# Attention kernel on one core: GpSimd adds the bias to the scores that come back from DRAM, VectorE takes their maximum

## What is computed

```python
def _L0_attn_ref(hidden_states, w_qkv, w_o):
    qkv = hidden_states @ w_qkv
    ...
    scores = jnp.einsum('bqhgd,bkhd->bhgqk', q, k) * scale
    bias = -slopes[:, :, None, None] * sqrt_dist
    bias = jnp.where(rel[None, None] >= 0, bias, -jnp.inf)
    attn = jax.nn.softmax(scores + bias[None], axis=-1)
    out = jnp.einsum('bhgqk,bkhd->bqhgd', attn, v).reshape(B, S, NH * D)
    return out @ w_o

x = x + _L0_attn_ref(_layernorm(x), w_qkv, w_o)
x = x + _L0_ffn_ref(_layernorm(x), weight, bias, centroids, assignments)
```

## Time and profile before

| | us |
|---|---|
| median of 3 executions (1272.35 to 1277.04) | 1273.97 |
| the profiled execution, device time | 1272.32 |
| the same, span of its trace | 1270.7 |
| TensorE's matmuls busy | 1238.5 (97%) |
| VectorE busy | 787.2 (62%) |
| ScalarE busy | 751.9 (59%) |
| GpSimd busy | 520.2 (41%) |

### The profile page before, as it was taken

One profiled execution on the slowest core, in us unless ns is written; L12 is line 12 of the kernel. 1 busy time (PEld: TensorE's weight loads), 2 busy tenths in 40 slices (PEclk: granted clock), 3 DMA queues, 4 the chain that ended last, 5 costly groups with the idle time before them and its releaser, 6 DMA issues.

```text
span 1270.7 us, 21113 instructions
## 1 busy us (share of the span) xinstructions
PE 1238.5 (97%) x5880; PEld 1029.3 (81%) x5880; DVE 787.2 (62%) x2086; ACT 751.9 (59%) x2171; POOL 520.2 (41%) x476
## 2 busy tenths in 40 slices
PE   9899999999999999999999999999999999999988
PEld 8688878887788878887888878888788878888777
DVE  7777656566555565656565566555655566668577
ACT  5776566565555656665556656664566566556443
POOL 4422636226342545226352455325452364233213
PEclk9899999999999999999999999999999999999999
DMA  5543535444453444444443444534444444523203
GB/s 199 178 132 123 161 119 182 140 135 142 152 173 123 141 160 154 157 140 132 165 155 118 161 160 149 166 124 149 142 155 149 138 160 154 168 83 116 92 9 133
DMA packets 205530, 180.71 MB, mean 142 GB/s; under 512 B 12096, under 2 KB 158784, under 8 KB 205504
## 3 DMA queue, kind: packets, MB, share of 16 engines
q1 hardware_dynamic: 199680, 162.04, 38.8%
q0 software_dynamic: 5824, 18.36, 4.9%
HBM read 101.45 MB, written 78.91 MB: 142 GB/s over the span
## 4 chain that ended last, share of the span: by engine, by line
issue 34%; PE 31%; POOL 21%; DVE 5%; ACT 4%; DMA 4%; POOLq 1%; SPq 0%; DVEq 0%; ACTq 0%
PE ps L1385 29%; POOL ring L592 11%; POOL wqkv_lo L551 2%; POOL wo_lo L551 2%; POOL v_lo L598 2%; POOL wqkv_hi L549 2%; ACT prob L765 1%; DMA vT<-turned_s 1%; PE ps L1405 1%; DMA turned<-ring_whole 1%; POOL wo_hi L549 1%; ACT prob L777 1%; POOL raw L557 1%; POOL raw L560 1%; DVE vT L1083 1%
## 5 line engine op out<-in xcount | busy, mean ns | idle before, releaser
L1385 PE MATMUL ps<-xnT,wqkv_hi 128*128 (+2 forms) x1560 | 483.3, 391 | 1.7 <-DVE kT L1005 1.3
L592 POOL TENSOR_TENSOR ring<-ring_whole,pT_hi 128x512 fp32r<-128x512 f32 x189 | 246.1, 1302 | 522.3 <-ACT pT_hi L756 522.0
L1385 PEld LDWEIGHTS ps<-xnT,wqkv_hi 128*128 128x128 f32 x1560 | 289.2, 188 | 67.4 <-DVE kT L1005 6.1
L1385 PE MATMUL ps<-xnT,wqkv_lo 128*128 (+1 forms) x780 | 303.3, 389 | 0.0
L765 ACT ACTIVATE prob<-prob,negmax 128x256 f32<-128x256 f32 (+1 forms) x384 | 177.1, 463 | 187.5 <-DVE negmax L1083 187.5
L1385 PE MATMUL ps<-wo_hi,oT_hi 128*128 128x512 f32 x512 | 200.1, 391 | 0.8 <-DVE acc L1062 0.8
L1385 PE MATMUL ps<-wo_lo,oT_hi 128*128 128x512 f32 x512 | 199.6, 390 | 0.0
L1385 PE MATMUL ps<-wo_hi,oT_lo 128*128 128x512 f32 x512 | 199.2, 389 | 0.0
L756 ACT ACTIVATE pT_hi<-ring_whole 128x512 fp32r<-128x512 f32 x189 | 118.0, 625 | 129.9 <-DMA ring_whole<-turned 88.3
L1062 DVE TENSOR_TENSOR acc<-ps,acc 128x512 f32 (+1 forms) x128 | 88.2, 690 | 146.6 <-PE ps L1385 146.2
L1385 PEld LDWEIGHTS ps<-xnT,wqkv_lo 128*128 128x128 f32 x780 | 146.9, 188 | 30.8
(11 more groups left out here) (155 smaller groups left out, 1788.4 us busy)
## 6 DMA issues: line engine op xcount, KB each, us to landing
turned<-ring_whole SPq DMA_DIRECT2D x189, 256.0 KB, 2.1
ring_whole<-turned SPq DMA_DIRECT2D x189, 256.0 KB, 2.9
turned_v<-vT SPq DMA_DIRECT2D x32, 256.0 KB, 2.0
...
```

The source lines that it names most:

```text
L592: pool.tensor_tensor(ring_slot(c), whole_slot(c), pT_hi[:, c % 2, :].bitcast(F32), ALU.subtract).then_inc(pT_lo_done, 1)
L1385: ins = pe.matmul(dst, l, r, start=start and m == 0, stop=stop and m == n - 1)
```

## The change

**GpSimd adds, VectorE takes the maximum.** For part 2 (`e` = 2 and 5) VectorE's four fused instructions go. GpSimd's new `sum_scores(u, b)` adds the bias in place to the returned piece, 128x512 in one instruction, and VectorE's new `find_max(u, b)` takes the four negated maxima in one `tensor_reduce`. Since the piece now has its own sign, `exps` for these parts has scale 1.0. GpSimd does `sum_scores(u, 0)` after `v_lo_part(u)` (in a fourth unit between the splits of the second and the third chunk of `w_qkv`), and `sum_scores(u - 1, 1)` between `pT_lo(1)` and `pT_lo(2)` of `body(u)`.

**Loads.** The loads of the third and fourth chunk of `w_qkv` go from GpSimd to SyncE. SyncE's loop over units becomes one over groups, with the two loads around `scores_in(v, 0)` of the fourth unit. Each waits until the slot is split. They have semaphores of their own.

**Orders.** VectorE: `find_max(u - 1, 1)` stands behind `turn(4)`, and `invert_sums(3)` follows it, ahead of `proj_lo(2)`; `turn(5)` goes behind `proj_lo(3)`. ScalarE: in unit 1 alone `pT_hi(0)` goes ahead of `exps(3)` and `exps(4)`; in the tail `pT_hi(1)` and `pT_hi(2)` move up, each ahead of a `normalise`. VectorE in the tail: the piece of `b = 1` is taken up after `dense_part(1, 1, 1)` and not ahead of `dense_part(1, 1, 0)`.

The diff, cut to its core (the rest declares semaphores and calls these functions in the first units, on the same pattern):

```diff
             def turn_first(v):
                 scores_out(v, 0)
                 scores_in(v, 0)
+                turn_rest(v)
+
+            def turn_rest(v):
                 scores_out(v, 1)
...
+            def last_qkv(g, c):
+
+                sp.wait_ge(raw_split, g * (2 * NC) + c - 1)
+                rows = w_qkv[c * P:(c + 1) * P, :]
+                kv = rows[:, NH * D:].rearrange("p (a n) -> p a n", a=2)[:, :, bass.ds(g * D, D)]
+                sp.dma_start(raw[:, c % 2, 0:HPG * D], rows[:, bass.ds(g * (HPG * D), HPG * D)]).then_inc(last_loaded[c % 2], 16)
+                sp.dma_start(raw[:, c % 2, HPG * D:QKV_W].rearrange("p (a n) -> p a n", a=2), kv).then_inc(last_loaded[c % 2], 16)
+
+            def unit(v):
+                turn_v(v)
+                turn_first(v)
+                turn_second(v)
+
+            def last_of_group(g):
+                v = g * QUADS + QUADS - 1
+                turn_v(v)
+                scores_out(v, 0)
+                last_qkv(g + 1, 2)
+                scores_in(v, 0)
+                last_qkv(g + 1, 3)
+                turn_rest(v)
+                turn_second(v)
...
-            with sp.Fori(1, UNITS - 3) as v:
-                turn_v(v)
-                turn_first(v)
-                turn_second(v)
+            for v in range(1, QUADS - 1):
+                unit(v)
+            last_of_group(0)
+            with sp.Fori(1, NKV - 1) as g:
+                for q in range(QUADS - 1):
+                    unit(g * QUADS + q)
+                last_of_group(g)
+            unit(UNITS - QUADS)
...
@@ split_qkv @@
                     if c == 2:
                         v_lo_part(g * QUADS - 1)
-
-                    pool.wait_ge(raw_loaded[c % 2], g * 96 - 96 + 32 * (c // 2 + 1))
+                        sum_scores(g * QUADS - 1, 0)
+
+                    if c < 2:
+                        pool.wait_ge(raw_loaded[c % 2], g * 64 - 32)
+                    else:
+                        pool.wait_ge(last_loaded[c % 2], g * 32)
                     split(raw[:, c % 2, :], wqkv_hi[:, c, :], wqkv_lo[:, c, :], g * (2 * NC) + SETUP + c + 1)
-                    if c < 2:
-                        load_after(g, c)
...
+            def sum_scores(u, b):
+
+                pool.wait_ge(s_in[b], u * 16 + 16)
+                pool.wait_ge(bias_ready, group_count(u))
+                by_head = score_tile(b).rearrange("p (i h c) -> p h i c", i=P // BLK, h=HPG)
+                pool.tensor_tensor(by_head, by_head, bias[:, :, P:SEQ].rearrange("p h (i c) -> p h i c", c=BLK),
+                                   ALU.add).then_inc(scores_summed, 1)
+
+            def pT_lo_first(u):
+                pT_lo_part(u, 0)
+                pT_lo_part(u, 1)
+                sum_scores(u - 1, 1)
+                pT_lo_part(u, 2)
...
             def plain_body(u):
-                for c in range(CHUNKS):
+                pT_lo_first(u)
+                for c in range(3, CHUNKS):
                     pT_lo_part(u, c)
                 v_lo_part(u)
+                sum_scores(u, 0)
...
@@ group @@
                     pT_lo_part(u + 1, h)
+                    if h == 1:
+                        sum_scores(u, 1)
...
@@ ScalarE @@
-                    ins = act.activation(s, s, ACT.Exp, bias=negmax[:, n:n + 1], scale=-1.0, accum_out=rowsum[:, n:n + 1])
+                    ins = act.activation(s, s, ACT.Exp, bias=negmax[:, n:n + 1], scale=1.0 if e % 3 == 2 else -1.0,
+                                         accum_out=rowsum[:, n:n + 1])
...
                 if attn:
+                    if is_second(u):
+                        pT_hi_part(u, 0)
                     exps(u - 1, 3)
                     exps(u - 1, 4)
-                    pT_hi_part(u, 0)
+                    if not is_second(u):
+                        pT_hi_part(u, 0)
...
@@ ScalarE, tail @@
             pT_hi_part(u, 0)
+            pT_hi_part(u, 1)
             normalise(u - 1, 2)
             exps(u - 1, 5)
-            pT_hi_part(u, 1)
+            pT_hi_part(u, 2)
             normalise(u - 1, 3)
             oT_hi_part(u, 0)
-            pT_hi_part(u, 2)
...
@@ VectorE @@
+            def find_max(u, b):
+
+                dve.wait_ge(scores_summed, u * 2 + b + 1)
+                n = 4 * (2 * b + 1)
+                dve.tensor_reduce(negmax[:, n:n + HPG], score_tile(b).rearrange("p (i h c) -> p h i c", i=P // BLK, h=HPG),
+                                  AX_XY, ALU.max, negate=True).then_inc(scores_biased, 1)
...
                     if attn and i == 0:
                         invert_sums(u - 1, 2)
-                        add_bias(u - 1, 5)
+                    if attn and i == 2:
+                        invert_sums(u - 1, 3)
...
                             turn(u - 1, 3)
                             turn(u - 1, 4)
-                            invert_sums(u - 1, 3)
-                        if i == 2:
+                            find_max(u - 1, 1)
+                        if i == 3:
                             turn(u - 1, 5)
...
```

54 lines of the change are left out of this document (28 added, 26 removed).

## The result

The changed kernel takes 1314.1 us (median of 4, 1311.2 to 1315.8) against 1274.25 before; the ratio is 1.0309, with a 95% interval of 1.0280 to 1.0337. Its profiled execution took 1312.8 us with a span of 1311.2, against 1270.7 before, so 40.5 us more span. The forecast was 1306.

A forecast was written before the change was run, and what follows sets the result against it. TensorE was taken as the bound, so only its waits count: 9.8 + 17.5 - 1.6 + 12 - 4.5 = +33 on the profiled 1272.3, so 1306 us; 8-in-10 range 1275 to 1328.

The forecast's parts named there:

- The chain of b = 1: GpSimd's addition, VectorE's maximum, then ScalarE's exps(5): in plain units exps(5) starts 3.0 us later, at 11.0 us into the unit.
- the wait at chunk 5: TensorE's wait for a unit's last chunk: in plain units ready 23.7 us into the unit, wanted at 23.15.
- Plain units: 13 loop units (3, 6, 7, 10, ... 27): 0.75 us more each, +9.8 us.
- Second units: Second unit of each group (5, 9, ... 29), with w_o splits on GpSimd: +2.5 us in 7 units, +17.5 us.
- Unit 29: Last of the 7 second units of a group, priced like the others at +2.5 us.
- First units: First unit of each group (4, 8, ... 28): loss of 2.5 instead of 2.73 us, -1.6 us in 7 units.
- leave the late last chunk: Unit 16: the change removes about 1.7 of 2.73 us lost, but TensorE's late last chunk (0.55 us wait) stays.
- the crowded transfer: First units: chunk 5's way through DRAM beside the w_o loads, taken as 3.8 us, between 2.0 alone and 4.9.
- Layer norm units: Units 1, 2, 30, 31: later exps(5) and chunk 5's transposition between two tiles, about +3.0 us each, +12 us.
- Tail: End of the kernel: new VectorE and ScalarE orders shorten TensorE's waits of 2.75 and 2.12 us, -4.5 us.
- Boundaries win: Rival, faster: the delay of exps(5) fits into slack, plain units cost nothing; 1254 or 1255 us; 10%.
- The clock falls too: Rival, slower still: the clock drops after waits in second and first units, +21 us in 14 units, 1327 us; 17%.

The follow-up runs named there:

- run 1: Changed kernel with GpSimd's b = 1 addition between pT_lo(0) and pT_lo(1) instead of behind pT_lo(1): 1287.6 us.
- run 3: Changed kernel with GpSimd's b = 1 addition ahead of pT_lo(1) and VectorE's find_max(1) ahead of proj_lo(1); turn(5) stays behind proj_lo(3): 1268.3 us.
- run 2: Changed kernel with VectorE's turn(5) back behind proj_lo(2) instead of proj_lo(3): 1290.0 us.
- run 10: Kernel before with the b = 1 addition on GpSimd, its maximum and the moved turn(5) alone; loads, b = 0 and most other orders as before: 1352.2 us.
- run 6: Kernel before with only the loads of the third and fourth w_qkv chunk moved from GpSimd to SyncE: 1256.3 us.
- run 8: Kernel before with only the new orders of unit 1 and of the tail: 1267.7 us.
- run 5: The kernel of run 3 with turn(5) behind proj_lo(2) again: 1259.4 us.

## Why the forecast was nearly right, point by point

**The chain of b = 1: right.** Its times fell within 0.4 us of the forecast, in plain and in second units. Runs 1 and 3 showed that the delay hangs on both orders, GpSimd's and VectorE's, and run 2 that the wait at chunk 5 needs the moved `turn(5)` too.

**Plain units: right**, +7.9 us for a forecast +9.8.

**Second units: right in kind, the term too small**, +23.3 us for +17.5. Six of them cost 2.76 on average for 2.5; three had the clock's dip, 1.25 us each, which I had only as a rival, and the three without it cost 2.1, so that the wait itself was priced 0.4 too high. Unit 29 was counted as one of seven at 2.5 us and cost 6.7: the step that failed is that I moved chunk 5 in SyncE's queue and did not ask what stands behind it there. In unit 29 that is four loads, and behind these the values; that and the rest of the chain cost about 3.2 us (run 10), and the clock's fall and a wait 0.55 us longer the other 3.5.

**First units: the wrong mechanism, the term small by luck.** -1.6 us forecast, -4.3 measured, but as the sum of two large terms: -17.9 for the loads part, by run 6, and 13.5 for the late exponentials. The step that failed is "leave the late last chunk". I had the last chunk's lateness as a matter of the crowded transfer, and gave the two load issues no price beyond that the splits come earlier. They held the splits by 4.05 us, and the late splits were what blocked the additions; run 6 has the crowded transfer too, and its last chunk is in time. The transfer itself was near the forecast: 3.3 us in the changed kernel's unit 16 for 3.8.

**Layer norm units: right in kind, too small**: +4.4, +5.2, +5.2 and, with the tail's gain of run 8 taken out, +2.8 for unit 31, together 17.7 for +12. The forecast had 0.7 us for the transposition before the second tile; run 3 against run 5 gives up to 3.1, since the tile then falls behind a low half and beside GpSimd, and in unit 2 the clock falls after it.

**Tail: right**, -4.4 by run 8 for -4.5, on the kernel before. Beside the `b = 1` part it wasn't measured alone: unit 31 takes 105.9 us with the tail's old order (run 10) and 97.5 in the changed kernel, so the division of unit 31 above is an estimate.

**Rivals.** "Boundaries win" missed because nothing put the addition earlier; runs 3 and 5 are what it would have been, 1268 and 1259 us. "The clock falls too" is partly true: three second units and units 2, 29 and 30 lost time to it, some 8 us in all (an estimate, from the 1.25 us of a second unit) where it had 21. The maximum beside GpSimd was never blocked, as the last section shows.
